# Building two adjacency tiles per chunk in the first edge stage, and gathering five tiles instead of six in the first weighted pass

## The reference

```python
def _L0_gnn_ref(x, pairlist, f_ij, f_ij_cutoff, ...):      # first edge stage
    h = x @ W_in
    Wij = ssp(f_ij[:, 0, :] @ W_f1 + b_f1) @ W_f2 + b_f2
    x_ij = h[idx_j] * Wij * f_ij_cutoff
    agg = jax.ops.segment_sum(x_ij, idx_i, num_segments=n_atoms)
    ...
def _L1_gnn_ref(...):      # attention: softmax over the edges of a node
def _L2_gnn_ref(...):      # unweighted sum over edges, then a matrix
def _L3_gnn_ref(x, edge_index, edge_weight, W0, b0, W1, b1, ...):
    def gcn_conv(x, src, dst, ew, W, b, n):
        h = x @ W
        norm = dinv[src] * ew * dinv[dst]
        return jax.ops.segment_sum(h[src] * norm[:, None], dst, num_segments=n) + b
    z = prelu(gcn_conv(z, src, dst, ew, W0, b0, n), prelu_w)     # first weighted pass
    z = prelu(gcn_conv(z, src, dst, ew, W1, b1, n), prelu_w)     # second weighted pass
    ...
```

## Time and profile before

| | |
|---|---|
| median of three runs | 5446.83 us |
| profiled execution, first to last instruction (its span) | 5443.9 us |
| span below the median of the runs | 2.9 us |
| PE busy | 4066.1 us (75%) |
| POOL busy | 3669.0 us (67%) |
| DVE busy | 2992.1 us (55%) |
| ACT busy | 1658.7 us (30%) |
| chain that ended last, largest parts | PE 41%, DMA 16%, issue 16%, DVE 13%, POOL 9% |

### The profile page before, as it was taken

The page is one execution under the profiler, slowest core; times in us unless marked ns, Lnnn a source line. Parts: engine busy times, 40 slices in busy tenths (PEclk is TensorE's granted clock), DMA queues, the critical chain, the costliest instruction groups (busy, mean ns, idle before and its releaser), DMA issues.

```text
span 5443.9 us, 87969 instructions
## 1 busy us (share of the span) xinstructions
PE 4066.1 (75%) x26225; PEld 3586.0 (66%) x26225; DVE 2992.1 (55%) x10663; ACT 1658.7 (30%) x3538; POOL 3669.0 (67%) x3340
## 2 busy tenths in 40 slices
PE   2767667777775488888887578886788889588886
PEld 1655555555554377777777466665677788488886
DVE  3655555555551677777777444445455444444445
ACT  2444444444442343333333322222211111111110
POOL 0788888888885277777773577761677777377773
PEclk8777777777777688888887899998899989799997
DMA  6666666666665222222221222210343434244442
GB/s 203 129 115 115 115 115 115 115 115 115 115 106 103 59 56 56 55 55 54 54 55 26 65 54 50 50 49 25 115 143 125 144 125 140 81 153 152 143 161 83
DMA packets 405518, 531.76 MB, mean 98 GB/s; under 512 B 136751, under 2 KB 321688, under 8 KB 398520
## 3 DMA queue, kind: packets, MB, share of 16 engines
q0 software_dynamic: 199680, 221.72, 23.3%
q1 hardware_dynamic: 205496, 305.85, 17.8%
HBM read 374.16 MB, written 153.13 MB: 97 GB/s over the span
## 4 chain that ended last, share of the span: by engine, by line
PE 41%; DMA 16%; issue 16%; DVE 13%; POOL 9%; DVEq 2%; SPq 1%; ACT 1%; POOLq 0%; ACTq 0%
DMA sums<-G,idx 15%; POOL sums L737 9%; PE psC L1225 8%; PE psF L1225 8%; PE psC L1158 4%; PE psE L1211 4%; PE psD L1211 4%; PE psA L1148 3%; DVE S L1748 3%; PE psB L1200 2%; PE psA L1200 2%; DVE early L1737 1%; DVEq L491 1%; DVE G L1654 1%; PE psD L1163 1%
## 5 line engine op out<-in xcount | busy, mean ns | idle before, releaser
L712 POOL DMA_INDIRECT G<-table,idx x1664 | 1596.0, 959 | 846.0 <-issue 495.4
L737 POOL DMA_INDIRECT sums<-G,idx x832 | 1283.7, 1543 | 370.6 <-issue 181.2
L694 POOL DMA_INDIRECT G<-table,idx x832 | 786.2, 945 | 288.0 <-issue 256.1
L970 ACT COPY arena<-psA 128x600 f32<-128x600 f32 x312 | 205.7, 659 | 1227.8 <-PE psA L1200 1183.1
L1098 PE MATMUL psE<-arena,stage 128*128 128x128 f32 x832 | 212.9, 436 | 444.3 <-ACT G L890 444.2
L1098 PEld LDWEIGHTS psE<-arena,stage 128*128 128x128 f32 x832 | 182.6, 323 | 528.9 <-ACT G L890 528.9
L1225 PE MATMUL psC<-arena,stage 128*128 128x144 f32 (+1 forms) x3822 | 510.6, 294 | 0.0
L1225 PEld LDWEIGHTS psC<-arena,stage 128*128 128x128 f32 x3822 | 498.6, 202 | 0.0
L1225 PE MATMUL psF<-arena,stage 128*128 128x144 f32 (+1 forms) x3822 | 494.0, 288 | 0.0
L1510 DVE TENSOR_TENSOR arena<-psB,G 128x1024 f32<-128x1024 f32 x104 | 127.4, 1225 | 647.8 <-PE psB L1079 647.8
L1225 PEld LDWEIGHTS psF<-arena,stage 128*128 128x128 f32 x3822 | 482.7, 197 | 0.0
(11 more groups left out here) (282 smaller groups left out, 7979.2 us busy)
## 6 DMA issues: line engine op xcount, KB each, us to landing
adjacency<-arena SPq DMA_DIRECT2D x26, 2400.0 KB, 8.5
arena<-adjacency SPq DMA_DIRECT2D x26, 2400.0 KB, 9.6
acc<-in_src_row SPq DMA_DIRECT2D x104, 512.0 KB
arena<-in_dst_row SPq DMA_DIRECT2D x104, 512.0 KB
G<-table,idx POOLq DMA_INDIRECT x2496
sums<-G,idx POOLq DMA_INDIRECT x832, 3.4
sums<-arena SPq DMA_DIRECT2D x4, 3300.0 KB, 26.4
table<-stage SPq DMA_DIRECT2D x28, 448.0 KB, 3.0
```

What stands on the lines that cost most here:

```text
L694: pool.indirect_dma_start(G[st.r][:, t * width:(t + 1) * width], None, tables[n], bass.IndirectOffsetOnAxis(ap=idx[st.r][:, t:t + 1], axis ...
L712: pool.indirect_dma_start(G[at.r][:, t * D:(t + 1) * D], None, tables[n], bass.IndirectOffsetOnAxis(ap=idx[at.r][:, t:t + 1], axis=0)).the ...
L737: pool.indirect_dma_start(sums_dram[t % SUMS], bass.IndirectOffsetOnAxis(ap=idx[st.r][:, t:t + 1], axis=0), G[st.r][:, t * TW:(t + 1) * TW ...
L970: A.copy(dense_at(at.g, m.loaded + j, k % GROUP), counts_in((k * m.built + j) % 2)).then_inc(mixed["kept"], 1)
```

## The change

Two dense tiles per chunk, tiles 0 and 1, are now built in the first edge stage, in `psE` half a plane at a time, and stored to memory there. Pass 3 no longer builds and stores two tiles: it loads them, builds a third, and gathers five, as pass 4 did already. A plane is now laid out chunk by chunk (600 numbers of a chunk side by side) rather than interleaved over four chunks, so a matmul of line 1225 reads its 144 columns in 12 runs of 12 numbers, where it read 3 runs of 48. Many one-use semaphores of DVE are merged into shared ones, since the program needs new ones elsewhere; the order of DVE's work is not changed by that. Cut to its core, where `half_kept` runs on ACT, `edge_counts` and the new wait behind `done_before` (it is in `low_sources_summed`) on PE, and `edge_hots` on DVE:

```diff
-    for n, what in ((2, (3, 0, False, True)), (3, (2, 0, True, False)), (4, (3, STORED, False, False))):
+    for n, what in ((2, (3, 0, True)), (3, (3, STORED, False)), (4, (3, STORED, False))):
...
-    adjacency = nc.dram_tensor("adjacency", [GROUPS, P, STORED * PLANE], F32, kind="Internal").ap()
+    adjacency = nc.dram_tensor("adjacency", [CHUNKS, P, STORED * KEYS], F32, kind="Internal").ap()
...
+        def columns_of(g, n, h):
+            return dense[g][:, 0:n * PLANE].rearrange("p (u h s) -> p u h s", h=HIS, s=SLOTS)[:, :, h, :]
...
+            def store_adjacency(st):
+                for j in range(STORED):
+                    sp.wait_ge(adj_kept[j], st.c * 2 + 2)
+                    sp.dma_start(stored_chunk(st.c, j), edge_planes[j]).then_inc(adj_out[j], 16)
...
-            walk(sp, general, l0["over"], [(load_edges, 0), (load_window, 0)], [load_edges], [], 0, steps=1)
+            walk(sp, general, l0["over"], [(load_edges, 0), (load_window, 0), (store_adjacency, ROWS)], [load_edges], [], ROWS,
+                 steps=1, near_end=adjacency_stored)
...
-                sp.dma_start(dense[at.g][:, 0:STORED * PLANE], adjacency_of(at.group)).then_inc(adj_moved[at.g], 16)
+                for t in range(m.loaded):
+                    sp.dma_start(dense[at.g][:, t * PLANE:(t + 1) * PLANE].rearrange("p (c x) -> p c x", c=GROUP),
+                                 stored_group(at.group, t)).then_inc(adj_in[at.g], 16)
...
+            def half_kept(j, half):
+                def stage_(st):
+                    act.wait_ge(adj_half[j], st.c * 2 + (half + 1))
+                    if half == 0 and not (isinstance(st.c, int) and st.c == 0):
+                        act.wait_ge(adj_out[j], st.c * 16)
+                    A.copy(edge_planes[j][:, half * (KEYS // 2):(half + 1) * (KEYS // 2)],
+                           psE[:, 0:KEYS // 2]).then_inc(adj_kept[j], 1)
+                return stage_
...
-            walk(act, general, l0["over"], [(sums_kept, 2), (filter_ssp, 0), (keep_rows, 0)], [rows_scaled, filter_ssp, sums_kept], [], 2,
-                 steps=1)
+            walk(act, general, l0["over"],
+                 [(sums_kept, 2), (half_kept(0, 0), 1), (filter_ssp, 0), (half_kept(0, 1), 1), (half_kept(1, 0), 1),
+                  (keep_rows, 0), (half_kept(1, 1), 1)],
+                 [rows_scaled, filter_ssp, sums_kept], [], 2, steps=1)
...
                 done_before(pe, l0["out"], st, 1)
+                if not st.general:
+                    pe.wait_ge(adj_kept[STORED - 1], st.c * 2 + 2)
...
+            def edge_counts(j, half):
+                def stage_(st):
+                    pe.wait_ge(adj_made[j], st.c + 1)
+                    if j == 0 and half == 0:
+                        if not (isinstance(st.c, int) and st.c == 0):
+                            pe.wait_ge(l0["out"], st.c)
+                    elif half == 0:
+                        pe.wait_ge(adj_kept[j - 1], st.c * 2 + 2)
+                    else:
+                        pe.wait_ge(adj_kept[j], st.c * 2 + 1)
+                    M.matmul(psE[:, 0:KEYS // 2], edge_lohots[j], edge_keyhots[j][:, half * (KEYS // 2):(half + 1) * (KEYS // 2)],
+                             start=True, stop=True).then_inc(adj_half[j], 1)
+                return stage_
...
-                 [(low_sources_summed, 2), (filter_one, 0), (high_sources_summed, 2), (filter_two, 1), (window_rows, 0)],
+                 [(low_sources_summed, 2), (filter_one, 0), (high_sources_summed, 2), (edge_counts(0, 0), 1), (filter_two, 1),
+                  (edge_counts(0, 1), 1), (edge_counts(1, 0), 1), (window_rows, 0), (edge_counts(1, 1), 1)],
...
-                        ins = M.matmul(segments((psC, psF)[at.g][:, 0:m.dense * SEG], m.dense), stage[:, h * D:(h + 1) * D],
-                                       segments(dense[at.g][:, 0:m.dense * PLANE], m.dense)[:, :, h * SEG:(h + 1) * SEG],
-                                       start=(h == 0), stop=(h == BLOCKS - 1))
+                        ins = M.matmul(segments((psC, psF)[at.g][:, 0:m.dense * SEG], m.dense * GROUP), stage[:, h * D:(h + 1) * D],
+                                       columns_of(at.g, m.dense, h), start=(h == 0), stop=(h == BLOCKS - 1))
...
+            dve.wait_ge(sums_clear, 16 * SUMS)
+            V.tensor_copy(edge_srclo, srcl[:, :])
             start_pass(0, "rows")
...
+            def edge_hots(j):
+                def stage_(st):
+                    at = bass.ds(st.c * TILES + j, 1)
+                    if not (isinstance(st.c, int) and st.c == 0):
+                        dve.wait_ge(adj_half[j], st.c * 2)
+                    V.tensor_scalar(edge_lohots[j], iota[:, :], edge_srclo[:, at], ew[:, at], ALU.is_equal, ALU.mult)
+                    V.tensor_scalar(edge_keyhots[j], iotak[:, :], key[:, at], None, ALU.is_equal).then_inc(adj_made[j], 1)
+                return stage_
...
-                 [(filter_sum, 1), (spread_window, 0), (same_source, 1), (scatter_indices, 1), (messages, 1)],
+                 [(filter_sum, 1), (edge_hots(1), 1), (spread_window, 0), (same_source, 1), (scatter_indices, 1), (messages, 1),
+                  (edge_hots(0), 0)],
```

More of the change, by code:

```diff
@@ L79, with __init__ @@
 class Mix:
-    def __init__(self, n, dense, loaded, stored, counts, chunks, before):
-        self.n, self.dense, self.loaded, self.stored, self.counts = n, dense, loaded, stored, counts
+    def __init__(self, n, dense, loaded, counts, chunks, before):
+        self.n, self.dense, self.loaded, self.counts = n, dense, loaded, counts
         self.built, self.thin, self.chunks = dense - loaded, TILES - dense, chunks
@@ L89, in __init__ @@
         self.spread0 = (before.spread0 + before.dense * chunks if before else 0) + 1
+        self.loads0 = before.loads0 + (16 * before.loaded * (chunks // TURN)) if before else 0
     def made(self, c, j):
@@ L98, in applied, with loads @@
         return group + self.index * (self.chunks // GROUP)
+    def loads(self, turns):
+        return turns * (16 * self.loaded) + self.loads0
     def rows(self, use):
@@ L313, in build_program @@
                 counted[m] += n
-        l0 = sems("l0", "pre abs exp ln ssp wij node_id spread rows rows_kept msg same compared "
-                        "away moved to idx summed_low summed out_low out src_kept gidx_f gidx gathered over")
+        l0 = sems("l0", "pre abs exp ln ssp wij node_id spread rows rows_kept msg same own "
+                        "to idx summed_low summed out_low out gidx_f gidx gathered over")
         rows_at = [sem(f"rows_at{r}") for r in range(ROWS)]
@@ L329, in build_program @@
         mixed = sems("mixed", "made counted kept applied spread")
-        adj_moved = [sem(f"adj_moved{g}") for g in range(2)]
+        adj_in = [sem(f"adj_in{g}") for g in range(2)]
+        adj_made = [sem(f"adj_made{j}") for j in range(STORED)]
+        adj_half = [sem(f"adj_half{j}") for j in range(STORED)]
+        adj_kept = [sem(f"adj_kept{j}") for j in range(STORED)]
+        adj_out = [sem(f"adj_out{j}") for j in range(STORED)]
         links = Counter(dve_link, 0)
@@ L623, in turn @@
                         sp.dma_start(idx[at.r][:, m.dense:TILES], a["src"][:, at.from_tile(m.dense)]).then_inc(midx[at.r], 16)
-                        if m.stored and k % GROUP == GROUP - 1 and not (at.first and at.g == 0):
-                            store_adjacency(m, Spot(i, 0) if at.g else Spot(i - 1, GROUP))
                         if m.loaded and k == 0 and at.first:
@@ L965, in turn @@
                         at = Spot(i, k)
-                        if m.stored and k % GROUP == 0 and not at.first:
-                            act.wait_ge(adj_moved[at.g], i * 16)
                         for j in range(m.built):
```

100 lines of the change are left out of this document (54 added, 46 removed).

## The result

| | before | after |
|---|---|---|
| median of the runs | 5449.09 us | 5789.29 us |
| lowest to highest, 4 runs each | 5442.59 to 5456.21 | 5778.95 to 5791.61 |
| ratio of after to before, 95% interval | | 1.0624 [1.0611, 1.0637] |
| span of the profiled execution | 5443.9 | 5777.1 |
| first edge stage, first to last scatter | 1568.0 | 2014.9 |

The changed kernel is 6.2% slower. The prediction was 5371, with a range of 5318 to 5465. The 5449.09 us before has one run more in it (5456.21) than the 5446.83 that the prediction started from.

The account below looks back on a forecast made before the run. POOL's chain of scatters was taken to bound the first edge stage at 15.10 us per chunk. Pass 3's -125 and the stage's +49 gave -76: span 5443.9 to 5368, plus 2.9 for the median, 5371 us; range 5318 to 5465.

Parts of the forecast that it names:

- the ring: First edge stage: PE and ACT take turns over `psE`; 14.30 us a turn at full clock, 15.55 forecast, stage +49 us.
- the ring's clock term: First edge stage: allowance for PE's lowered clock after idle time, 1.25 us per turn, with ends 0 and 2.5.
- a sign that its ring is wrong: First edge stage: `filter_two` ending after `filter_ssp`, or 300-column copies far from 0.41 us, would show the predicted turn wrong.
- rival B: First edge stage: PE's clock stays low and lengthens the turn to 17.6 us; stage +260, kernel 5582 us; chance 0.16.
- Pass 3: Pass 3 becomes pass 4 in its counts, 624 gathers falling to 520; gain 125 us, 105 to 135 possible.
- The two loads per group: Passes 3 and 4: two DMAs per group of four chunks instead of one, issued one group ahead; cost 0.
- Rival D: Matmuls of line 1225: short runs cost time; 5446 us at a tenth of the bound, some 6100 at all; chance 0.04.
- D's bound: Matmuls of line 1225: upper limit for nine more runs, 0.095 us each time, 728 us in all; 0 was taken.
- A: First edge stage: POOL stays the bound and the stage does not grow; kernel 5322 us; chance 0.20 together with C.
- C: First edge stage: stores delay POOL's scatters, 0.36 us a chunk, 38 in all; kernel 5360 us; chance 0.20 with A.
- The small terms: First edge stage: 300-column copy 0.41 us; DVE's one-hots and SP's stores cost 0; later start 0 to 25 us, 0 taken.

Follow-up runs that it names:

- e4: Changed kernel plus eight unread 128 x 128 matmuls on PE ahead of the low sums, all waits kept; 5402.04 us, one run.
- e10: e3 plus four unread matmuls on PE behind `window_rows`, ahead of the low sums; 5352.38 us, 0.9822 of the kernel before.
- e8: e7 with each store made a second time, into a tensor nobody reads; 5355.9 us, 0.9835 of the kernel before.
- e5: Changed kernel with each store made a second time, into a tensor nobody reads; 5705.3 us, one run.
- e3: Changed kernel with the last half plane ahead of `window_rows` and its copy ahead of `keep_rows`; 5388.52 us, 0.9875 of the kernel before.
- e9: e3 plus eight unread matmuls on PE behind `window_rows`, ahead of the low sums; 5384.42 us, 0.9889 of the kernel before.
- e7: e3 plus two unread matmuls in each of the two idle times between half planes; 5386.51 us, 0.9878 of the kernel before.
- e1: Changed kernel with half planes in their own bank, two ring waits cut, three DVE operands in SBUF; 5391.38 us, 0.9881 of the kernel before.
- e2: Changed kernel with half planes in their own bank and three DVE operands in SBUF, all waits kept; 5775.12 us, one run.
- e6: Changed kernel with the edits of e1 and e3 joined; 5403.63 us, 0.9926 of the kernel before.

## Why the prediction was wrong

**The failed step is the ring's clock term, 1.25 us** ("I take half of it, 1.25; both ends, 0 and 2.5, stay"). Set beside the measured turn of 19.22 us, and beside the turn of e4 from 704.19 us on, which is the same ring at full clock, my terms were, in us:

| part of the ring | priced | changed kernel | e4 |
|---|---|---|---|
| `keep_rows` and last copy, to the low sums | 2.42 | 729.32 - 726.79 = 2.53 | 2.61 |
| low sums | 0.99 | 1.06 | 1.06 |
| `filter_one` | 1.91 | 2.62 | 1.91 |
| high sums and their copy | 1.74 | 716.62 - 713.78 = 2.84 | 1.93 |
| first half plane to the issue of the third | 5.29 | 724.49 - 716.62 = 7.87 | 5.41 |
| `window_rows`, to `keep_rows` | 1.95 | 2.30 | 2.31 |
| sum | 14.30 | 19.22 | 15.23 |

The structure was right: which engines, which waits, which order. At full clock it takes 15.2 us (e4), so hand-overs that I had not priced cost 0.9. The rest of the mean turn, 19.42 - 15.2 = 4.2 us, is clock, where I had 1.25 and at most 2.5. Set against e4's mean pace of 15.8, in which the clock still lapses here and there, the gain is 3.6. Both errors point the same way, and the ring had only 0.8 us to spare against POOL.

The largest part, 7.87 - 5.41 = 2.46 us, lies where the path changed engine. I had ACT's `filter_ssp` (3.30) outlast PE's `filter_two` (2.66). At half clock `filter_two` took 4.96 us, and ACT waited 1.75 us for the half plane behind it. The prediction had named this as a sign that its ring is wrong, and the clock at 0.74 or below with the stage over 1700 us as the sign of rival B; both came.

Why the term was too small: I took it from two blocks behind one idle time in another pass and stopped counting there. Behind 1.48 us of idle time these took 1.95 us each and behind 2.31 us 2.76 and 3.62, which is (2.76 - 1.95) + (3.62 - 1.95) = 2.5 more; the ring's 2.0 us lies between, and half of 2.5 was an estimate. No run shows 1.25 us for the ring; the runs showed the 4.2 us above. In the ring the low clock covers `filter_one`, the high sums, the half plane and `filter_two`, half the turn. The kernel before would have warned me only in part; its clock came back inside `filter_two`, at 717.2, and the low sums and `filter_one` ran at full clock (1.00 from 720.69 to 723.6 us). PE of the kernel before:

```profile
716.84 0.57 PE L1079 MATMUL psB<-early,arena 128*128 128x128 f32 x2
717.24 0.22 PE L1078 MATMUL psB<-bf_rows,ones 128*128 128x128 bf16 x1
...
720.69 1.06 PE L1089 MATMUL psE<-arena,stage 128*128 128x128 f32 x8
721.68 1.98 PE L1057 MATMUL psA<-acc,early 21*128 21x512 f32 x4
```

**Rival B was the mechanism**, at 0.16: "PE's clock stays as low as it is and the ring pays for it". It too was under-priced: 3.2 us for the clock where it was 4.2, and none for hand-overs, so 17.6 us a turn and 5582. Its argument against did not hold: PE did have more work and a shorter longest idle time, 2.4 us instead of 4.2, and the clock was 0.72 all the same.

**Pass 3** gave 115 us, within 105 to 135, where 125 was taken. Its 520 gathers and 496.41 us of POOL are pass 4's. The two loads per group cost nothing that shows, as forecast: pass 4, which has them too, kept its 695 us.

**Rival D** fell. Line 1283 (1225 before) alone in passes 3 and 4 of the changed kernel, busy time of PE and PEld:

```profile
4274.00:4979.00 705.00, 346.94 (x2548) 337.69 (x2548) 0.92 0.45 142
5031.00:5726.00 695.00, 351.76 (x2548) 342.88 (x2548) 0.91 0.46 143
```

That is 0.136 and 0.138 us each, against 0.137 with long runs. That more columns take PE longer shows elsewhere: two matmuls of 300 columns took 1.17 us, four of 128 took 1.06. (A tenth of D's bound, 73 us, would have given 5444 and not 5446.)

**Rivals A and C.** Neither came about in the changed kernel, since POOL was not the bound. In e10, where it is, the pace is 15.3 and the total 5352, between A's 5322 and C's 5360. C's 0.36 us looks right in size, but e8 carries twice the stores at the same 15.3: if stores cost the first 0.2 us, doubling them did not cost it again. About 0.1 of the 0.2 us are longer scatters (1.543 us on the mean before, 1.553 in e10, 1.557 in e8, eight a chunk); the rest stayed open, and so did what lengthens them.

**The small terms** held: a copy of 300 columns took 0.41 us in the median, DVE's one-hots stayed hidden (DVE waits 467 us for `filter_two`), and the first scatter came 6.7 us later, within 0 to 25. SP's stores held nobody up: doubled in e5, they cost nothing.

## What to carry to other kernels

When an order of hand-overs between two engines gets close to the time of the bound, price its whole turn at the clock that the stage has, not at the clock of its best stretch, and add the hand-overs; if the ring at that clock is above the bound, expect it to set the pace. Do not leave an engine idle behind a long row of another one when a short independent piece can go first: moving a 0.41 us copy ahead of a 2.01 us row was worth 394 us here. If PE must wait in such a ring, unread matmuls (matmuls whose result nobody reads) in the idle time can pay, but only in the right place and no more of them than the ring has room for: here four ahead of the low sums took the median from 5388.52 to 5352.38 us (e3, e10), eight there to 5384.42 (e9), four between the half planes to 5386.51 (e7).

## What the runs showed of the hardware

- PE's granted clock does not follow its busy time. The changed kernel's window has 81% busy (891.61 of 1100 us) at 0.72; e4's has 86% at 0.95; e7's has 92% at 0.83. A low clock itself makes the same work busy for longer (the high sums took 2.08 us at 0.50 in the changed kernel, and 1.16 at 1.00 in e4), so a busy share is not an amount of work.
- The clock can stay low while PE works almost without a break. In the changed kernel the granted clock was 0.50 from 712.3 to 722.0 us, from inside `filter_one` to the last matmuls of `filter_two`, with one idle time of 0.77 us.
- Four unread matmuls per turn ahead of the low sums took the clock from 0.83 to 0.93 (e3, e10); four in the short idle times between half planes left it at 0.83 (e7).
- With the stores doubled the clock was higher (0.75 against 0.72, 0.86 against 0.83, one trace each) and both kernels were faster. The cause is open.
- In the three kernels with DVE's moved operands in SBUF (e1, e2, e6) up to one scatter per turn took over 2 us instead of 1.54 (mean 1.62 to 1.65 against 1.55), always beside a DVE row that read a moved operand: the one of 1.23 us over 1024 columns or one of the eight of 0.35 us behind it. Beside the same rows with the operand in PSUM it stayed at 1.54 to 1.56. No run moved the operands without the half planes' bank.
